# A graph layer with a routed mixture of experts on one core: pacing of the router gathers, one-hot comparisons read from PSUM, and two weight matrices side by side

## The reference

```python
xn = layernorm(x)
# graph layer: mean of the neighbours' rows, one linear layer, unit length
summed = segment_sum(xn[src], dst);  deg = segment_sum(1, dst)
agg = summed / maximum(deg, 1)[:, None]
g = concatenate([xn, agg]) @ weight
g = g / norm(g) + bias
# linear attention of 8 heads: k and v normalised by head
dots = einsum('hnd,hne->hde', k, v)          # over all nodes
m = einsum('hnd,hde->hne', q, dots) / n @ Wout.T + bout
x = x + g + m
# experts: a graph attention over other 131,072 edges gives 4 scores a node
scores = mean over heads(layernorm(attention_aggregate(layernorm(x)) + b_gat))
top 2 of 4 -> softmax -> gate
x = x + sum_e gate[e] * (gelu(x2 @ W1[e] + b1[e]) @ W2[e] + b2[e])   # x2 = layernorm(x)
```

## Time and profile before

| | us |
|---|---|
| median of 3 runs | 4531.07 |
| the profiled execution's own time | 4539.89 |
| its span | 4538.1 |

### The profile page before, as it was taken

One profiled execution on the slowest core, in us unless ns is written; L12 is line 12 of the kernel. 1 busy time (PEld: TensorE's weight loads), 2 busy tenths in 40 slices (PEclk: granted clock), 3 DMA queues, 4 the chain that ended last, 5 costly groups with the idle time before them and its releaser, 6 DMA issues. The chain is left out here.

```text
span 4538.1 us, 48378 instructions
## 1 busy us (share of the span) xinstructions
PE 3283.0 (72%) x13336; PEld 2287.7 (50%) x13338; DVE 2082.7 (46%) x4748; ACT 831.4 (18%) x2082; POOL 3050.2 (67%) x3009
## 2 busy tenths in 40 slices
PE   0118888888888677777777747999999999995000
PEld 0115555555555465665666634666666666663000
DVE  8884555555555355444444420223222223232667
ACT  5301222222221011111111112222222222221000
POOL 2627777777777777777777776777777777763310
PEclk6559999999999799989889878999999999997555
DMA  6204444444444456666656522222222222222766
GB/s 197 97 28 125 126 126 125 124 125 125 125 126 114 124 157 180 165 165 165 160 158 161 152 54 66 64 65 76 67 65 75 64 71 67 72 59 89 226 209 221
DMA packets 378958, 540.08 MB, mean 119 GB/s; under 512 B 117898, under 2 KB 295402, under 8 KB 378727
## 3 DMA queue, kind: packets, MB, share of 16 engines
q0 software_dynamic: 119136, 234.44, 22.9%
q1 hardware_dynamic: 259719, 304.59, 20.6%
HBM read 392.03 MB, written 146.74 MB: 119 GB/s over the span
## 5 line engine op out<-in xcount | busy, mean ns | idle before, releaser
L790 POOL DMA_INDIRECT rows<-xn_rows,gsrc x1664 | 1726.7, 1038 | 542.8 <-issue 497.9
L1260 POOL DMA_INDIRECT nb<-route_rows,idx x1024 | 1013.7, 990 | 312.0 <-issue 312.0
L1014 PE MATMUL PS<-rows,oh 128*128 128x257 f32 x3328 | 858.1, 408 | 210.1 <-DMA rows<-xn_rows,gsrc 209.2
L1014 PEld LDWEIGHTS PS<-rows,oh 128*128 128x128 f32 x3328 | 641.0, 200 | 346.8 <-DMA rows<-xn_rows,gsrc 243.8
L1576 PE MATMUL PS<-x2g,arena 128*128 128x500 f32 x1600 | 679.5, 585 | 46.7 <-DMA x2g<-x_turned 44.2
L1584 PE MATMUL PS<-arena,hid 128*125 128x256 f32 x3200 | 697.5, 380 | 20.9 <-ACT hid L1549 20.9
L1584 PEld LDWEIGHTS PS<-arena,hid 128*125 128x125 f32 x3200 | 598.5, 188 | 129.6 <-issue 33.1
L1523 DVE TENSOR_TENSOR y_sb<-PS,b_b 125x512 f32<-125x512 f32 x200 | 128.6, 685 | 1059.8 <-PE PS L1584 1059.5
L1576 PEld LDWEIGHTS PS<-x2g,arena 128*128 128x128 f32 x1600 | 305.7, 191 | 406.3 <-issue 357.9
L1549 ACT ACTIVATE hid<-PS,b_sb 128x500 f32<-128x500 f32 x400 | 270.9, 677 | 616.5 <-PE PS L1576 616.5
L1088 PE MATMUL PS<-wg,p_t 128*125 128x256 f32 x400 | 161.1, 492 | 245.4 <-issue 131.4
(11 more groups left out here) (301 smaller groups left out, 3607.7 us busy)
## 6 DMA issues: line engine op xcount, KB each, us to landing
y_rows<-y_sb SPq DMA_DIRECT2D x100, 512.0 KB, 2.7
arena<-y_rows SPq DMA_DIRECT2D x100, 512.0 KB, 4.9
rows<-xn_rows,gsrc POOLq DMA_INDIRECT x1664
nb<-route_rows,idx POOLq DMA_INDIRECT x1024
sum_rows<-kept SPq DMA_DIRECT2D x104, 128.5 KB
x_rows<-x SPq DMA_DIRECT2D x100, 128.0 KB, 4.1
hid<-x_rows SPq DMA_DIRECT2D x100, 128.0 KB, 8.3
m_in<-sum_rows SPq DMA_DIRECT2D x100, 125.5 KB
```

Source lines behind the costliest of these rows:

```text
L790: pool.indirect_dma_start(out=rows[w][h][:, q, 0:D], out_offset=None, in_=xn_rows, in_offset=bass.IndirectOffsetOnAxis(ap=gsrc[:, s * HU + ...
L1014: last = mm(SUM[:, 0:D + 1], oh[w][h][:, q, :], rows[w][h][:, q, :], start=h == 0 and q == 0, stop=h == 1 and q == HU - 1)
L1260: pool.indirect_dma_start(out=nb[b % NBUF][:, c, :], out_offset=None, in_=route_rows, in_offset=bass.IndirectOffsetOnAxis(ap=idx[:, b * W ...
```

## The change

It has four parts.

1. In the router block, a constant `AHEAD = 4`: gather c of a batch waits until the gather four before it has landed, on one of four semaphores used in turn; DVE waits for all four of them ahead of `scores`.
2. The numbers 0 to 127 are copied once into a bank of PSUM (`NUMBERS`), and `one_hot` and `hist` read them there and no longer from SBUF. Their count, sizes and places stay.
3. To free that bank, a tile's keys have one bank, `KP`, and no longer two in turn. `keys_values` of tile j waits until ACT has copied the keys of tile j-1 (before: j-2). Some other results move to other banks.
4. `wg` and `mix` become `own_w` (own-row half of `wg` at columns 0 to 255, `mix` at 256 to 511) and `mean_w`. `linear` is four matmuls in place of six, two of them 512 columns wide. The load of `wg` becomes two.

```diff
+AHEAD = 4
...
-        wg = gb("wg", [P, 4, D])
-        mix = gb("mix", [P, 2, D])
+        own_w, mean_w = gb("own_w", [P, 2, 2 * D]), gb("mean_w", [P, 2, D])
...
-                sp.dma_start(wg[:], gnn_w.rearrange("(k p) f -> p k f", p=P)).then_inc(s_w, 16)
+                sp.dma_start(own_w[:, :, 0:D], gnn_w[0:D, :].rearrange("(k p) f -> p k f", p=P)).then_inc(s_w, 16)
+                sp.dma_start(mean_w[:], gnn_w[D:2 * D, :].rearrange("(k p) f -> p k f", p=P)).then_inc(s_w, 16)
...
-            SUM, XT, CNT, DT, KP, VP = PS[0], PS[1], PS[2], PS[3], PS[4:6], PS[6:8]
-            UP, MP = PS[4:6], PS[6]
-            ST, GM, X2, H = PS[1], PS[4:6], PS[6], PS[7]
+            SUM, XT, CNT, DT, KP, VP = PS[0], PS[1], PS[2], PS[3], PS[4], PS[6:8]
+            NUMBERS = PS[5][:, 0:P]
+            UP, MP = (PS[4], PS[7]), PS[6]
+            ST, GM, X2, H = PS[1], PS[3:5], PS[6], PS[7]
...
+                v.tensor_copy(NUMBERS, iota_j[:])
...
-                    v.tensor_tensor(oh[w][h][:], iota_j[:].rearrange("p (o n) -> p o n", o=1).broadcast_to([P, HU, P]),
+                    v.tensor_tensor(oh[w][h][:], NUMBERS.rearrange("p (o n) -> p o n", o=1).broadcast_to([P, HU, P]),
                                     along(rel[h][:], P), ALU.is_equal).then_inc(s_ohr[h], 1)
...
-                                                   iota_j[:, 0:n].rearrange("p (o n) -> p o n", o=1).broadcast_to([P, 4, n]),
+                                                   NUMBERS[:, 0:n].rearrange("p (o n) -> p o n", o=1).broadcast_to([P, 4, n]),
...
-                    wait_after(pe, s_kc, j - 1)
+                    wait_after(pe, s_kc, j)
                     for k in range(2):
-                        mm(KP[u][0:NP, :], x_t[u][:, k * NP:(k + 1) * NP], wkv[:, k, 0:INNER], start=k == 0, stop=k == 1)
+                        mm(KP[0:NP, :], x_t[u][:, k * NP:(k + 1) * NP], wkv[:, k, 0:INNER], start=k == 0, stop=k == 1)
...
                     wait_after(pe, s_x1, j)
+                    both = lambda k: mm(GM[u][0:NP, :], p_t[u][:, k * NP:(k + 1) * NP], own_w[:, k, :], start=k == 0, stop=k == 1)
+                    both(0)
                     for k in range(2):
-                        xk = p_t[u][:, k * NP:(k + 1) * NP]
-                        mm(G, xk, wg[:, k, :], start=k == 0, stop=False)
-                        mm(G, s_t[u][:, k * NP:(k + 1) * NP], wg[:, 2 + k, :], start=False, stop=k == 1)
-                    for k in range(2):
-                        last = mm(MX, p_t[u][:, k * NP:(k + 1) * NP], mix[:, k, :], start=k == 0, stop=k == 1)
-                    last.then_inc(s_lin, 1)
+                        mm(GM[u][0:NP, 0:D], s_t[u][:, k * NP:(k + 1) * NP], mean_w[:, k, :], start=False, stop=False)
+                    both(1).then_inc(s_lin, 1)
...
                     for c in range(W):
+                        if b or c >= AHEAD:
+                            pool.wait_ge(s_nb[c % AHEAD], (b * W + c) // AHEAD * 16)
                         pool.indirect_dma_start(out=nb[b % NBUF][:, c, :], out_offset=None, in_=route_rows,
                                                 in_offset=bass.IndirectOffsetOnAxis(ap=idx[:, b * W + c:b * W + c + 1], axis=0)
-                                                ).then_inc(s_nb[b % NBUF], 16)
+                                                ).then_inc(s_nb[c % AHEAD], 16)
...
-                    dve.wait_ge(s_nb[b % NBUF], (b // NBUF + 1) * 16 * W)
+                    for q in range(AHEAD):
+                        dve.wait_ge(s_nb[q], (b + 1) * 16 * W // AHEAD)
```

More of the change, by code:

```diff
@@ L348, in _ @@
                 v.tensor_copy(gplan[:, SPANS:SPANS + 2], small[0:1, 41:43])
-                dve.wait_ge(s_w, 9 * 16)
+                dve.wait_ge(s_w, 10 * 16)
                 heads = wkv.rearrange("p k (h e) -> p (k h) e", e=DH)
@@ L873, in mixed @@
                     dve.wait_ge(s_mixp, 4)
-                    v.tensor_copy(mix[:], MP[:, :].rearrange("p (k f) -> p k f", k=2)).then_inc(s_mixd, 1)
+                    v.tensor_copy(own_w[:, :, D:2 * D], MP[:, :].rearrange("p (k f) -> p k f", k=2)).then_inc(s_mixd, 1)
                 def places(_, t, u, w):
@@ L962, in squares @@
                     wait_after(act, s_ss, j)
-                    a(sq[:, 0, :], KP[u][0:NP, :], ACT.Square)
+                    a(sq[:, 0, :], KP[0:NP, :], ACT.Square)
                     a(sq[:, 1, :], VP[u][0:NP, :], ACT.Square).then_inc(s_sq, 1)
                     act.wait_ge(s_dt, j + 1)
-                    a(k_sb[u][:], KP[u][0:NP, :], ACT.Copy).then_inc(s_kc, 1)
+                    a(k_sb[u][:], KP[0:NP, :], ACT.Copy).then_inc(s_kc, 1)
                 def roots(j, _, u, w):
@@ L1081, in linear @@
                 def linear(j, _, u, w):
-                    G, MX = GM[u][0:NP, 0:D], GM[u][0:NP, D:2 * D]
                     pe.wait_ge(s_stc, j + 2)
@@ L1153, in build @@
             s_adf = ev("s_adf")
-            s_nb = [ev(f"s_nb{q}") for q in range(NBUF)]
+            s_nb = [ev(f"s_nb{q}") for q in range(AHEAD)]
             s_nbf = ev("s_nbf")
```

## The result

| | before | changed |
|---|---|---|
| median of 4 runs each | 4530.46 us (4526.44 to 4531.96) | 4421.08 us (4418.25 to 4423.60) |
| the profiled execution | 4539.89 (span 4538.1) | 4423.44 (span 4421.7) |

The ratio on record is 0.9742, with a 95% interval from 0.9722 to 0.9762; the quotient of the two medians above, 0.9759, lies in it. The changed kernel is faster by 109.4 us in the medians and by 116.4 us between the two profiled executions. The forecast was 4422 us.

A forecast was written before the change was run, and what follows sets the result against it. POOL's gathers, held while DVE reads two tensors from SBUF, set the first 112 steps' pace. 4539.9 - 110 + 0.2 = 4430 us for the profiled execution, 4531 - 109 = 4422 for the median, range 4406 to 4438.

The forecast's parts named there:

- The numbers in PSUM: Graph block, first 112 steps: the 896 gathers take 1120 us instead of 1232.7, 110 us less after 3 for leftovers.
- The second part: Graph block from step 112, 768 gathers: a loop through the store of `rt` sets the pace, so the gain is 0.
- PE's wait for rows: Graph block, first 112 steps: PE's wait for gathered rows falls from 194 to about 95 us.
- One bank for the keys: Graph block: ACT's copy ends 4.5 us before PE's next keys begin, so sharing one bank costs 0.
- weights side by side: `linear` in the graph block: the same columns stream, at best 0.2 us a step; counted as 0.
- Four under way: Router block: gathers land in under 5.0 us but for the first few, 2 us in all, covered; cost 0.
- A: Graph block, first 112 steps: DVE's single-input operations also hold gathers, giving 29 us back, 4451 us; chance 0.11.
- B: Graph block's second part: freed gathers gain there too, up to 40 us; half of it gives 4402 us; chance 0.09.
- C: Graph block's comparisons: their broadcast form, not the operand's memory, holds gathers, so nothing is freed, 4531 us; chance 0.04.
- D: Router block: gathers landing in 5.5 us stall POOL with four under way, +124 against -109, 4546 us; chance 0.04.

The follow-up runs named there:

- the third chip: The changed kernel run once more, unaltered, on a third chip (kernel before there: 4546.70 us): 4420.37 us, ratio 0.9730.

## Why the prediction was right

**The numbers in PSUM: right, mechanism and size.** The step said 110 us from the first 896 gathers, of 112.7 possible; 112.1 came. Their mean is 946 ns, the undisturbed value, and step 112's gathers start at 1445.7 (forecast some 1449). Only 0.6 of the 3 us left for leftovers was needed. Taking this part alone gives all of the gain, and taking it back alone gives all of it away.

**The second part: right at 0, with the reason shown.** The 36.8 us of freed gather time became 39.9 us of wait for PE; 84.1 us were measured where about 80 were forecast. That the loop through the store of `rt` sets that pace was read from the earlier trace rows; four buffers for `rt` show it, 45 us. The 768 gathers of the second part, in one and the same code, took 1036.0 us in the profiled execution of the result and 1021.6 in that on the third chip. The forecast's own range had allowed for such a shift, 107 steps of 0.15 us. So that the median came within 1 us of the forecast is luck; within some 15 us is what the working could give. Why the profiled execution before took 9 us more than its median, and 116 us were gained between the profiled ones for 109 in the medians, is not shown: no trace of another execution before was kept.

**PE's wait for rows: off in size.** The forecast was about 95 us, and it was 118.5, because PE's own work shrank from 9.15 to 8.84 us a step with the granted clock of 0.98. The end didn't hang on it.

**One bank for the keys, weights side by side: right at 0.** The keys' wait doesn't appear, and the kernel without the numbers but with all else stands at 0.9984 (to 1.0004). Six matmuls or four for `linear` made no difference on the one chip where that was tried alone, the slow one. The traces elsewhere agree: with six (the numbers alone) the 768 gathers of the second part took 1023.3 us, with four between 1021.6 and 1036.0.

**Four under way: right at 0 in the time, but one sign of being wrong came up.** The prediction would be wrong, it said, if POOL showed waits for landings beyond the first dozen gathers. POOL shows 24 such waits, 13.9 us in all, and they run on to the 993rd of the 1024 gathers. The sum, then one of the last:

```profile
POOL nb L1262 <- DMA nb<-route_rows,idx: 13.9, 24, 2.9
```

```profile
3911.88 0.94 POOL L1262 DMA_INDIRECT nb<-route_rows,idx  x1 [0.47 <-DMA nb<-route_rows,idx]
```

Forecast were some 2 us at the first gathers. They are more, because gathers over 5 us do occur: by the trace's semaphore events one lands 2.41 us after its start in the median, but 8 of the 1016 that can be read take over 5, up to 7.3. From the first router gather to the end of the last it takes 1330.9 us where it took 1325.4. Of the 7.0 us between the last gather and its batch, 5.5 went to the waits and the rest to the landing: DVE waits 0.30 us there, as the last row of the router block shows. The chain that ended last shows it too: before, it ran through PE's experts, and now the router gathers on POOL (L1262) are 16.0% of it. It cost nothing that shows in the time, since PE's wait at the end of the experts is 2.7 us and was 2.6, but nothing was left. Two under way show the price on the other side of the edge.

**The rivals.** A, gathers held by DVE's single-input operations: not in the first 112 steps, where it was to cost 29 us. L826, the operation it was worked out from, holds none, and the mean has no room for it (946 ns over 896). But the mechanism is real, and the reason given against it, that DVE pays and not POOL, is only half of it. In the second part of the changed kernel 9 gathers end 0.82 us behind an operation of DVE with one input tensor in SBUF, 7 behind `second_norm` (L928) and 2 behind `mean` (L840), and 26 behind an addition of two tensors in SBUF in `residual` (L918), which the change had left as it was:

```profile
1490.66 0.43 DVE L918 TENSOR_TENSOR x<-x,bias_x 125x256 f32<-125x256 f32 x1
1490.72 1.18 POOL L792 DMA_INDIRECT rows<-xn_rows,gsrc  x1 [0.30 <-issue]
...
1495.79 0.41 DVE L928 TENSOR_SCALAR x<-x,mv,rstd 125x256 f32<-125x256 f32 x1
1495.95 1.07 POOL L792 DMA_INDIRECT rows<-xn_rows,gsrc  x1 [0.30 <-issue]
```

They cost 3.7 us in `residual` and 0.7 in the others. Where the gather came first, DVE's one-input operations went on varying as in the earlier trace rows, L840 from 0.35 to 0.59 us. The Trainium skill (SBUF — State Buffer, "Who interferes with whom") says that a two-port operation of DVE and one of GpSimd block each other whoever comes second; both halves appear here. The same section takes an operation with both inputs in SBUF to contend with GpSimd's reads, and infers that the making of descriptors isn't touched by it. Here it is touched: 0.82 us of each held gather wait for the end of such an operation, and that was the whole case. B, a gain in the second part: no, by POOL's wait. C, the form and not the memory: no, by the runs with the same form and other memories. D: not at four, real at two.

## What to carry to other kernels

Where POOL sends indirect DMAs without a pause, look at the operations on DVE that read two tensors from SBUF: put one of the two into PSUM, whichever is easier, and count the gain as the difference of a gather's mean to its undisturbed value, as long as no other loop sets the pace. Free all such operations at once, since the held time of one in the old trace isn't its share of the gain. Then look for the next loop in the waits for stores to land: two buffers whose store lands about 4 us behind its issue cost 45 us here, against four.

## What the runs showed of the hardware that was not expected

- A held gather ends 0.814 to 0.828 us behind the end of the DVE operation that holds it (259 gathers in the first 112 steps of before), whatever that one's length (0.57, 0.67 or 1.22 us). It is held only if that operation began first. A gather that nothing holds takes 0.95.
- Between comparisons with two inputs in SBUF and gathers the holding goes one way. The comparisons of 1024 results lasted 1.22 to 1.23 us in the mean with their inputs in SBUF or in PSUM, and 1.22 in the median also where the gather had begun first. With DVE's one-input operations either can wait: a gather took 1.07 us behind L928, and L840 took up to 0.59 beside a gather for 0.35 alone.
- With two gathers under way, two leave in 3.02 us, more than the median landing of 2.41. A part of the difference is that a waiting gather starts 0.26 us behind the landing it waits for (median of 657). By this a wait begins with four under way at a landing of some 4.7 us, and not the 5.0 of the prediction. The rest of the difference is not accounted for.
- One chip of those used ran all kernels 28% slower, with idle time on ACT up to 10.51 us, and a limit of two under way made the kernel faster there. The cause is open.
